# Chained segment attention: two kinds of small products as 64-row pairs, fillers in two places of a step, another order of the first phase

## The reference

```python
def step(carry, seg):
    mem, z = carry
    qq, kk, vv = seg
    sigma_q = jax.nn.elu(qq) + 1.0
    scores = jnp.einsum('bhsk,bhtk->bhst', qq, kk) / scale
    scores = jnp.where(causal_mask, scores, -jnp.inf)
    att_dot = jax.nn.softmax(scores, axis=-1) @ vv          # local attention
    att_mem = sigma_q @ mem / (sigma_q @ z)                 # read of the memory
    sigma_k = jax.nn.elu(kk) + 1.0
    delta = vv - sigma_k @ mem / (sigma_k @ z)
    mem_new = mem + jnp.einsum('bhsk,bhsv->bhkv', sigma_k, delta)
    z_new = z + sigma_k.sum(axis=-2, keepdims=True).transpose(0, 1, 3, 2)
    att = beta * att_mem + (1.0 - beta) * att_dot
    out = att.reshape(Bsz, SEG, H * DV) @ Wo
    return ((mem_new, z_new), out)
```

## Time and profile before

| | us |
|---|---|
| median of 3 runs (2043.0 to 2052.14) | 2045.21 |
| profiled execution | 2052.14 |
| its span in the profile | 2050.4 |
| PE, DVE, ACT busy | 1785.6, 1044.2, 882.1 |
| PE busy, `write_memory` (L2087) and `read_memory` (L2097) | 86.5 and 94.4 |
| PE busy, `local_attention` (L2121) and `turn_reads` (L2135) | 61.5 and 58.9 |

### The profile page before, as it was taken

One profiled execution on the slowest core, in us unless ns is written; L12 is line 12 of the kernel. 1 busy time (PEld: TensorE's weight loads), 2 busy tenths in 40 slices (PEclk: granted clock), 3 DMA queues, 4 the chain that ended last, 5 costly groups with the idle time before them and its releaser, 6 DMA issues. The chain is left out here.

```text
span 2050.4 us, 27324 instructions
## 1 busy us (share of the span) xinstructions
PE 1785.6 (87%) x9347; PEld 1447.8 (71%) x9347; DVE 1044.2 (51%) x2075; ACT 882.1 (43%) x1698; POOL 244.2 (12%) x237
## 2 busy tenths in 40 slices
PE   5988786987689999999877969969889989988898
PEld 4676544765568888887635758758888878878855
DVE  2266436234445555455565345554655565556466
ACT  3466324332244333433774343353444354344434
POOL 2010002212022222221101112220000000000000
PEclk8999996988789999999898979977999999999989
DMA  2000030110033433342100124220000000000100
GB/s 103 6 15 10 0 132 1 39 31 0 18 106 108 117 115 107 113 118 66 52 0 19 28 73 115 65 72 1 16 16 0 15 15 15 0 15 0 40 0 20
DMA packets 47074, 91.49 MB, mean 45 GB/s; under 512 B 7697, under 2 KB 24081, under 8 KB 46810
## 3 DMA queue, kind: packets, MB, share of 16 engines
q1 hardware_dynamic: 47026, 90.89, 14.7%
HBM read 89.52 MB, written 1.35 MB: 44 GB/s over the span
## 5 line engine op out<-in xcount | busy, mean ns | idle before, releaser
L438 PE MATMUL bank<-l1m_src_hi,l1m_w_hi 128*128 128x512 f32 x384 | 150.4, 392 | 7.5 <-DVE l1m_src_lo L507 7.5
L2234 ACT ACTIVATE l_mem<-bank 128x129 f32<-128x129 f32 x240 | 62.3, 279 | 217.1 <-PE bank L2087 216.3
L438 PE MATMUL bank<-l1m_src_hi,l1m_w_lo 128*128 128x512 f32 x384 | 150.1, 391 | 0.0
L438 PE MATMUL bank<-l1m_src_lo,l1m_w_hi 128*128 128x512 f32 x384 | 150.1, 391 | 0.0
L410 POOL TENSOR_TENSOR l1m_w_lo<-l1m_w,l1m_w_hi 128x512 fp32r<-128x512 f32 x96 | 104.8, 1109 | 325.5 <-ACT l1m_w_hi L475 325.5
L514 DVE TENSOR_TENSOR l1m_a<-l1m_s,bank 128x512 f32<-128x512 f32 x96 | 66.1, 688 | 116.6 <-ACT l1m_s L487 116.6
L491 ACT ACTIVATE l1m_a_hi<-l1m_a 128x512 fp32r<-128x512 f32 x96 | 60.7, 632 | 146.6 <-DVE l1m_a L520 146.6
L2368 DVE RECIPROCAL l_inv<-bank 128x1 f32<-128x1 f32 x240 | 39.2, 164 | 146.8 <-PE bank L2097 145.2
L2097 PE MATMUL bank<-l_mem,l_sg 128*128 128x129 f32 x480 | 94.4, 318 | 14.3
L2087 PE MATMUL bank<-l_dr,l_nkt 128*128 128x129 f32 x480 | 86.5, 302 | 21.7 <-issue 20.9
L528 DVE TENSOR_TENSOR l1m_a_lo<-l1m_a,l1m_a_hi 128x512 fp32r<-128x512 f32 x96 | 66.5, 692 | 70.8 <-ACT l1m_a_hi L491 70.8
(11 more groups left out here) (538 smaller groups left out, 4471.0 us busy)
## 6 DMA issues: line engine op xcount, KB each, us to landing
l1m_w<-in_l1f_win SPq DMA_DIRECT2D x48, 256.0 KB, 2.9
l1m_wr<-l1f_token_weights SPq DMA_DIRECT2D x32, 384.0 KB, 3.4
l1m_wr<-l1f_token_weights SPq DMA_DIRECT2D x32, 256.0 KB, 3.8
l_w<-in_l_w SPq DMA_DIRECT2D x9, 768.0 KB, 4.4
wmod<-in_wmod SPq DMA_DIRECT2D x4, 1536.0 KB, 9.8
l1m_w<-in_l1f_wout SPq DMA_DIRECT2D x48, 128.0 KB, 3.0
l1m_wr<-l1f_token_weights SPq DMA_DIRECT2D x32, 128.0 KB, 3.1
l2e_wr<-l2f_token_weights SPq DMA_DIRECT2D x16, 256.0 KB, 3.9
```

What stands on the lines that cost most here:

```text
L438: last = pe.matmul(k.bank[:, 2 * c + part, :], wq[:, half, at:at + P], xq[:, b, chunk(c)], start=(b == 0 and q == 0), stop=(b == DB - 1 an ...
L2234: act.activation(mem[:, a, (n + 1) % 2, 0:W1], k.bank[:, MEM + a, 0:W1], ACT.Identity).then_inc(s["mem_copied"], 1)
```

## The change

`local_attention(a)` and `turn_reads` issue each product on the 64 rows that hold its data; the even and the odd segment go to different banks (`2 + o`, `2 * a + o`) and follow each other, and both heads' results are read back by half (`att_by_half`). `local_attention` is now one piece of 16 products per head, at steps 8 and 11. `turn_reads` goes by tile: tiles 0 to 4, 5 and 6 of head 0 at steps 10, 12 and 14, tiles 0 to 5 and 6 of head 1 at steps 13 and 14; the last tile of both heads is turned between the first and second chunk of the next pair's projections. The output projection gives three matmuls ahead of a step's writes and two behind them in steps 1 to 6, the rest in step 7; `turn_probs` is split in the same way. In the first phase `scores(0)` moves between the two halves of the values, ScalarE leaves the odd half of head 0's turned keys to VectorE and places keys by chunk, and VectorE's `total`, `normalize` and `read_scores(1)` move into steps 1 to 8.

```diff
-    Y_AT = (0, 5, 10, 15, 20, 24, 28, 32)
+    Y_PARTS = 32
+    LAST = TT - 1
...
+        att_by_half = k.h[:].rearrange("p a (t o q) -> p a o t q", o=2, q=S)
...
+                def turn_reads(i, a, begin, end):
+
+                    if begin == 0:
+                        for o in range(2):
+                            pe.wait_ge(s["dot_scaled" if a else "pt_copied"], i * 4 + (2 + o + 1))
+                    if begin == LAST:
+                        pe.wait_ge(s["reads_added"], i * 8 + (2 * a + 2))
+                    for t in range(begin, end):
+                        pe.wait_ge(s["delta_ready"], i * CHAIN + (HP * 2 * t + a + 1))
+                        for o, half in enumerate((ODD, EVEN)):
+                            last = pe.matmul(k.bank[:, 2 * a + o, t * S:(t + 1) * S], dr[half, a, 2 * t + o, 0:P],
+                                             turn[half, half], start=True, stop=True)
+                    if end >= LAST:
+                        last.then_inc(s["turned"], 1)
...
-                            for o in range(2):
-                                at = (t % 4) * P + o * S
-                                last = pe.matmul(k.bank[:, 2 + c, at:at + S], v[:, t, a, o, :],
-                                                 pt[:, a, t, o * S:(o + 1) * S], start=True, stop=True)
+                        for t in range(TT):
+                            for o, half in enumerate(HALF):
+                                last = pe.matmul(k.bank[:, 2 + o, t * S:(t + 1) * S], v[half, t, a, o, :],
+                                                 pt[half, a, t, half], start=True, stop=True)
...
-                    def turn_reads(a, c, segments):
...
-                            last = pe.matmul(k.bank[:, 2 * c + a, at:at + S], dr[:, a, n, 0:P], turn[:, HALF[1 - n % 2]],
-                                             start=True, stop=True)
...
+                    def before_write(n):
+                        if n <= 6 and not first:
+                            project_out(i, 5 * n - 5, 5 * n - 2)
+                        if n == 7:
+                            if not first:
+                                project_out(i, Y_PARTS - 2, Y_PARTS)
+                            turn_probs(0, 0)
+                        if n == 8:
+                            local_attention(0)
+                        if n == 9:
+                            turn_probs(1, 0)
+                        if n == 10:
+                            turn_reads(i, 0, 0, 5)
+                        if n == 11:
+                            local_attention(1)
+                        if n == 12:
+                            turn_reads(i, 0, 5, 6)
+                        if n == 13:
+                            turn_reads(i, 1, 0, 6)
+                        if n == 14:
+                            turn_reads(i, 0, 6, LAST)
+                            turn_reads(i, 1, 6, LAST)
+
+                    def after_write(n):
+                        if n <= 6 and not first:
+                            project_out(i, 5 * n - 2, 5 * n)
+                        if n == 7:
+                            turn_probs(0, 1)
+                        if n == 9:
+                            turn_probs(1, 1)
...
-                    projections(0)
-                    values()
+                    projections(0, (0,))
+                    if not first:
+                        for a in range(HP):
+                            turn_reads(i - 1, a, LAST, TT)
+                    projections(0, (1, 2, 3))
+                    values(0)
                     scores(0)
+                    values(1)
                     keys_by_token(0)
-                    projections(1)
+                    projections(1, range(4))
...
                     for j in range(4):
                         queries_keys(j)
-                    place_keys(0)
+                    for c in range(NCH):
+                        place_keys(0, c)
                     values_copy(0)
+                    exponential(0)
                     values_copy(1)
-                    exponential(0)
                     keys_copy(0)
+                    act.wait_ge(s["v_even_copied"], i * 2 + 1)
+                    act.activation(dr[:, :, 0, 0:P], v[:, 0, :, 0, :], ACT.Identity, scale=-1.0
+                                   ).then_inc(s["first_ready"], 1)
                     for j in range(4, 8):
                         queries_keys(j)
                     keys_copy(1)
-                    act.activation(dr[:, :, 0, 0:P], v[:, 0, :, 0, :], ACT.Identity, scale=-1.0
-                                   ).then_inc(s["first_ready"], 1)
-                    place_keys(1)
+                    place_keys(1, 0)
                     for n in range(NS - 1):
                         for a in range(HP):
                             mem_copy(n, a)
-                        if n == 2:
+                        if n == 0:
+                            place_keys(1, 1)
+                        if n in (2, 4) and not final:
+                            high_part(i + 1, (n - 2) // 2)
+                        if n == 5:
                             exponential(1)
-                        if n in (3, 5) and not final:
-                            high_part(i + 1, (n - 3) // 2)
-                        if n in (8, 10):
+                        if n in (7, 9):
                             for c in range(NCH):
-                                probs_copy((n - 8) // 2, c)
-                        if n in (9, 11):
-                            dot_scale(0, (n - 9) // 2)
-                        if n in (12, 13):
-                            dot_scale(1, n - 12)
+                                probs_copy((n - 7) // 2, c)
+                        if n in (8, 11):
+                            dot_scale((n - 8) // 3)
...
+                def add_reads(i, a, begin, end):
+
+                    dve.wait_ge(s["turned"], i * 4 + ((3 if end == TT else 1) + a))
+                    dve.wait_ge(s["dot_scaled"], i * 4 + 4)
+                    for o in range(2):
+                        rows = att_by_half[:, a, o, begin:end, :]
+                        dve.scalar_tensor_tensor(rows, k.bank[:, 2 * a + o, begin * S:end * S].rearrange(
+                            "p (t q) -> p t q", q=S), bt[:, 0, a:a + 1], rows, ALU.mult, ALU.add
+                            ).then_inc(s["reads_added"], 1)
...
-                    for j in range(4):
-                        sigma(j)
+                    for j in range(2):
+                        sigma(j)
+                        if j == 0 and not first:
+                            for a in range(HP):
+                                add_reads(i - 1, a, LAST, TT)
...
                     values_copy(0)
-                    values_copy(1)
                     read_scores(0)
                     largest(0)
                     shift(0)
-                    for j in range(4, 6):
-                        sigma(j)
-                    total(0)
-                    normalize(0, 0)
-                    normalize(0, 1).then_inc(s["probs_ready"], 1)
-                    for j in range(6, 8):
+                    values_copy(1)
+                    keys_copy(0)
+                    for j in range(4, 7):
                         sigma(j)
                     keys_copy(1)
-                    read_scores(1)
+                    sigma(7)
                     for n in range(1, NS):
                         for a in range(HP):
                             delta(n, a)
                         if n == 1:
+                            read_scores(1)
+                        if n == 2:
                             largest(1)
-                        if n == 2:
+                        if n == 3:
+                            total(0)
+                        if n == 4:
                             shift(1)
-                        if n == 4:
+                        if n == 5:
+                            normalize(0, 0)
+                        if n == 6:
+                            normalize(0, 1).then_inc(s["probs_ready"], 1)
                             total(1)
-                        if n == 5:
+                        if n == 7:
+                            if not first:
+                                add_projection(i)
                             normalize(1, 0)
...
+                        if n == NS - 2:
+                            add_reads(i, 0, 0, LAST)
+                    add_reads(i, 1, 0, LAST)
```

122 lines of the change are left out of this document (42 added, 80 removed).

## The result

The changed kernel takes 1976.4 us (median of 4 runs, 1971.5 to 1979.0); the kernel before, run beside it, 2048.1 (2043.0 to 2052.1). The ratio is 0.9648, with a 95% interval of 0.9615 to 0.9681. The forecast was 1971, in a range from 1956 to 2022.

What follows compares the result with a forecast made beforehand. TensorE, busy 87% of the span, and its waits in the attention pairs were taken as the bound; savings of 57 (six middle pairs), 9.5 (first) and 7.9 (last), together 74.4, took the median 2045.2 to 1971 us, range 1956 to 2022.

Steps and rivals of the forecast that it cites:

- Price of a pass: Local attention and turned reads on TensorE: two alternating 64-row passes in 0.11 us, 7.0 us less work a pair of heads.
- Price of a change: TensorE going into or out of 64-row products: 0.1 us each, bounds 0 and 0.2, 14 changes a pair, 1.4 us.
- steps 10, 11, 13 and 14: Chain steps with turned reads or local attention as filler: forecast 3.3, 3.26, 3.07 and 2.0 us.
- Steps 1 to 6: Chain steps with six output-projection passes ahead of the write and four behind: 2.27 us each in place of 2.42.
- Step 7: Chain step with the rest of the projection and the turned probabilities: 2.57 us, with 0.3 spilling over from VectorE.
- First phase: From a pair's start to its first read: 23.8 us in place of 26.6, 4.7 of waits removed, some new ones added.
- Rival (b): First phase: its wait only moves, 2.8 us at one place, and the clock falls every second pair; 1999 us, chance 0.08.
- Middle pairs: Six middle pairs of heads: 60.5 us each against a mean of 70.0, together 57 us less.
- First pair: First pair of heads, no projection to fill with: stays at half clock, gains the tail and the wait, 9.5 us.
- Last pair and end: Last pair of heads up to its closing projection: from 72.2 to about 64.3 us, 7.9 less.
- Rival (c): Chain steps: lighter steps let the clock fall, slower than before, up to 157 us more, 2128 us; chance 0.06.
- The range: Whole kernel: 1956 to 2022 us, holding the forecast's own 1956 to 1992 and the rivals at 1999 and 2021.

Runs made afterwards that it cites:

- the experiment with two waits less: Changed kernel with the last tile's turned reads behind the second chunk of projections and VectorE's softmax work spread anew over steps 3 to 8: 1971.5 us, ratio 0.9608.
- the busy end: Kernel of the experiment with two waits less, plus 5, 10 and 6 idle transposes in the three waits ahead of the closing projection: 1969.7 us, ratio 0.9615.

## Why the prediction was right, point by point

The profiled executions stand 2050.4 and 1972.7 us long, 77.7 apart. From the first pair's start to the closing projection it was 567.3 us (1353.52 to 1920.84 in the earlier trace rows) and is 492.8 (1347.38 to 1840.15): 74.5 less, against 74.4 forecast. The other 3.2 are 6.1 less ahead of the stage, where nothing was changed, and 2.9 more behind it. Without the first, 71.6 are left, and the medians stand 71.7 apart. That the sum came out is luck: inside the 74.5 two errors of 5 us cancel. The mechanisms of the middle pairs were right, that of the first pair was wrong.

- **Price of a pass.** Forecast 0.055, measured 0.054. To read it from the scores of the earlier trace rows, where the halves are columns and not rows, was right. Rows alone, which the earlier trace rows stood for, bring nothing, 0.112 within a half, as the experiment with one half at a time shows. Right, and for the reason given: the loads of alternating halves start in twos, 0.007 apart, those within a half never under 0.109. Whether it needs the two banks as well was not tested.
- **Price of a change.** Forecast 0.1 each, the mean if coming out were free. Measured 0.20 in and 0.20 out; the upper bound was the value. Taken from the earlier trace rows as 0.2 for both ways, step 11 would have been 3.46 (measured 3.43). Mis-sized, worth about 0.45 us a pair: steps 10, 11, 13 and 14 are 0.04, 0.17, 0.15 and 0.09 late. In steps 8 and 10 the change in lies in the wait for ScalarE, and step 12 hides both.
- **Steps 1 to 6.** 2.27 forecast and measured; the undone split gave 2.42 back. Right.
- **Step 7.** Forecast 2.57 with 0.3 of spill from VectorE, measured 2.81. VectorE's timeline ahead of the write at 1569.71, which waits 0.32 for it (first fence of weight loads above), shows the normalization, the sum with its reciprocal, and only then the delta's:

```profile
1567.33 0.69 DVE L2392 TENSOR_TENSOR ln_square<-l_sc,l_st 64x512 f32<-64x512 f32 x1
1568.06 0.69 DVE L2387 TENSOR_REDUCE l_st<-l_sc 128x8 f32<-128x512 f32 x1
1568.77 0.20 DVE L2388 RECIPROCAL l_st<-l_st 128x8 f32<-128x8 f32 x1
1569.10 0.17 DVE L2398 RECIPROCAL l_inv<-bank 128x1 f32<-128x1 f32 x1
```

From the normalization to the delta's reciprocal 1.77 us pass. The read starts at 1568.02, so the reciprocal could have started at 1568.55, which leaves 1.22: 0.55 late. The prediction's own numbers, 1.65 of work in 1.25, give 0.40 and not the 0.3 that it wrote. Taken away in the experiment with two waits less, it gave 0.55. The mechanism was named, its size was half.
- **First phase.** 23.8 forecast and measured, the new waits 0.54 and 0.34 for 0.45 and 0.3, and 0.36 at the last tile for 0.6. Rival (b) is refuted: no wait of over 1 us is left. What the order is worth was shown by putting it back: 3.5 us a pair at full clock, and the fall of the clock in some pairs.
- **Middle pairs.** 61.3 for 60.5, six of them 52.0 in place of 57. The step that failed is the price of a change together with the spill, 0.7 of the 0.8.
- **First pair.** Forecast 9.5 less, at half clock as now; measured 75.22 - 60.55 = 14.7. The prediction took the half clock for a property of a pair with nothing to fill its steps. The experiments show that for such a pair the wait ahead of the steps decides: with waits of 0.61 us at most it kept 1.00, with one of 0.97 it didn't (64.86), and idle passes in the long wait kept it again. This failed step gave 5.2 us and paid for the middle pairs.
- **Last pair and end.** 7.9 forecast and measured. Behind it 3.0 us are lost in two rows (10.07 for 8.76 and 5.01 for 3.32), which no step of the prediction had: in place of one wait of 1.42 there are three, 0.55, 1.25 and 0.76, and the clock, which fell at this place before as well, stays low for longer. Shown by the busy end.
- **Rival (c).** Wrong for this kernel: steps with little work keep 1.00. In the two kernels that ran the halves one after the other the clock did fall, but under back-to-back passes, not for want of work.
- **The range.** The terms named for it, 8, 9 and 4 us, give 1992 above, but only 1963 with cheaper changes below; what led to 1956 is not said. Nothing hung on it.

## What to carry to other kernels

Products with a contraction of 64 are worth running on half the rows if consecutive ones alternate between the two halves and write to two banks: two passes in the time of one. In a row on one half they save nothing and can cost the clock. Whether the two banks are needed was not tested. Gather them in few places, since each visit costs 0.4 us for the way in and out, nearly four full passes, unless it lies in a wait. Price a wait of TensorE not by its length alone but also by the clock of what follows, the more where little work follows it. Idle passes put into the wait held the clock here.

## What the runs showed of the hardware

- Half-height passes one after the other let the granted clock fall from 2.4 to 1.2 GHz in the middle of a gapless series (1.00, then 0.50 from 1532.00 on), and 0.52 in the 17.8 us behind another, where the alternating ones stand at 1.00 with the same waits. I had taken only idle time for a cause. That the fall belongs to the half of the array that stands still is likely and was not shown, and the kernels that fell also wrote to one bank at a time.
- 64-row passes in a row on one half start 0.112 us apart, as with all 128 rows; with the halves in turn two start 0.007 apart, every 0.112. Where 16 passes of one half were followed by 16 of the other, four of the second half started early, between the last ones of the first.
- Idle passes in two waits of 1.93 and 2.78 us a pair of heads brought 12.7 us in the rows; a wait of 0.97 us ahead of a light stretch went with 4.3 us more in the first pair, 3.7 of them in its steps; the same wait ahead of fuller steps left the clock at 1.00.
- Pairs of halves into one and the same bank were not tried.
